# Local attention in a fused kernel: the third projection of values from step 14 to step 13, in another bank of PSUM

## The reference

```python
def _layer(x, wqkv, qs, ksc, wo, lg, lb, w1, b1, w2, b2):
    h = shift_token(x)
    q, k, v = jnp.split(h @ wqkv, 3, axis=-1)          # 8 heads of 64 each
    q = l2norm(q) * qs
    k = l2norm(k) * ksc
    q, k = rotary_xpos(q, k)
    o = local_attention(q, k, v)                       # window of 64: own block and the one before
    x = x + o @ wo
    h = shift_token(x)
    h = (h - mu) / jnp.sqrt(var + 1e-05) * lg + lb
    h = h @ w1 + b1
    a, g = jnp.split(h, 2, axis=-1)
    h = a * jax.nn.gelu(g, approximate=False)
    return x + h @ w2 + b2
```

## Time and profile before

| | |
|---|---|
| Runs | 4749.75, 4752.04, 4779.65 us |
| Profiled execution, its own time | 4754.64 us |
| Its span (first to last instruction) | 4752.8 us |
| Granted clock of TensorE, mean | 0.909 |
| Busy: PE, DVE, ACT, POOL | 4180.9, 3024.0, 2452.0, 1123.8 us |
| Chain that ended last: PE, DVE, ACT | 61%, 23%, 8% |

### The profile page before, as it was taken

The page is one execution under the profiler, slowest core; times in us unless marked ns, Lnnn a source line. Parts: engine busy times, 40 slices in busy tenths (PEclk is TensorE's granted clock), DMA queues, the critical chain, the costliest instruction groups (busy, mean ns, idle before and its releaser), DMA issues.

```text
span 4752.8 us, 62689 instructions
## 1 busy us (share of the span) xinstructions
PE 4180.9 (88%) x23278; PEld 1996.8 (42%) x23280; DVE 3024.0 (64%) x6690; ACT 2452.0 (52%) x4189; POOL 1123.8 (24%) x1579
## 2 busy tenths in 40 slices
PE   8888879999898889999886778989988989889999
PEld 5222335556522236555552235555553334333343
DVE  4888466777488867776346984666666653466622
ACT  3487634555348864554346543444444663236642
POOL 1100123333210013332113651111131013420034
PEclk8799988999779998998788998999987999969999
DMA  1100002111010011111000000000001000000000
GB/s 50 27 15 15 34 12 73 33 35 38 16 45 16 15 50 37 37 32 26 5 7 5 0 8 8 8 16 9 16 33 28 22 8 1 29 22 22 14 0 9
DMA packets 48017, 104.07 MB, mean 22 GB/s; under 512 B 15064, under 2 KB 15064, under 8 KB 46432
## 3 DMA queue, kind: packets, MB, share of 16 engines
q1 hardware_dynamic: 46560, 98.49, 7.6%
q10 hardware_dynamic: 1152, 1.57, 0.1%
HBM read 40.24 MB, written 1.05 MB: 9 GB/s over the span
## 4 chain that ended last, share of the span: by engine, by line
PE 61%; DVE 23%; ACT 8%; POOL 3%; issue 2%; DMA 1%; ACTq 1%; SPq 0%; POOLq 0%; DVEq 0%
PE PS L447 29%; PE PS L1123 8%; PE PS L1071 7%; DVE SM L1197 6%; PE PS L1103 3%; PE PS L2643 2%; DVE AR L2447 2%; ACT AR L454 2%; DVE AR L451 2%; PE PS L1756 1%; PE PS L1746 1%; PE PS L474 1%; PE PS L1076 1%; ACT AR L1171 1%; ACT PS L2391 1%
## 5 line engine op out<-in xcount | busy, mean ns | idle before, releaser
L1197 DVE TENSOR_REDUCE SM<-PS 128x1 f32<-128x512 f32 (+3 forms) x1792 | 1028.4, 626 | 242.7 <-PE PS L1071 161.9
L447 PE MATMUL PS<-AR,WS 128*128 128x512 f32 (+1 forms) x2112 | 1049.9, 636 | 76.2 <-DVE AR L451 30.3
L1171 ACT ACTIVATE AR<-PS 128x1024 f32<-128x1024 f32 (+3 forms) x896 | 825.5, 933 | 344.2 <-PE PS L1106 171.6
L454 ACT ACTIVATE AR<-PS 128x512 f32<-128x512 f32 (+4 forms) x728 | 440.1, 614 | 515.4 <-PE PS L447 387.9
L1071 PE MATMUL PS<-AR 51*128 51x512 bf16 (+3 forms) x1792 | 528.5, 392 | 142.1 <-DVE SM L1197 98.4
L447 PEld LDWEIGHTS PS<-AR,WS 128*128 128x128 f32 (+1 forms) x2112 | 400.1, 201 | 535.8 <-issue 407.2
L1827 ACT ACTIVATE AR<-PS,SM 128x128 f32<-128x128 f32 x512 | 229.6, 452 | 447.2 <-DVE SM L1890 443.2
L1123 PE MATMUL PS<-AR 128*32 128x512 f32 (+3 forms) x3584 | 452.2, 578 | 1.3 <-ACT AR L1171 0.9
L1071 PEld LDWEIGHTS PS<-AR 51*128 51x128 bf16 x1792 | 130.2, 94 | 662.6 <-DVE SM L1197 476.1
L1103 PE MATMUL PS<-AR 51*128 51x512 bf16 (+3 forms) x1792 | 388.1, 368 | 11.8 <-ACT AR L1171 11.0
L1230 POOL CAST MBT<-SM 128x8 bf16<-128x8 f32 x128 | 28.0, 219 | 1264.6 <-DVE SM L1201 1067.8
(11 more groups left out here) (323 smaller groups left out, 7153.8 us busy)
## 6 DMA issues: line engine op xcount, KB each, us to landing
TP<-RAW SPq DMA_DIRECT2D x512, 64.0 KB, 2.0
AR<-AR SPq DMA_DIRECT2D x720, 32.0 KB
WS<-wall SPq DMA_DIRECT2D x4, 3654.5 KB, 11.0
WS<-wall SPq DMA_DIRECT2D x8, 902.5 KB, 4.5
WS<-wall SPq DMA_DIRECT2D x2, 3334.5 KB, 10.5
WS<-wall SPq DMA_DIRECT2D x1, 2384.0 KB, 8.8
WS<-wall SPq DMA_DIRECT2D x1, 1543.5 KB, 6.0
AR<-AR ACTq DMA_DIRECT2D x48, 32.0 KB
```

Of the source, the lines that this page charges most:

```text
L447: t = e.matmul(o, l, r, start=(n == 0), stop=(n == len(pairs) - 1))
L454: return e.activation(o, i, ACT.Copy, scale=1.0)
L1171: e.activation(pv[:, :, off:512], sv[:, :, off:512], ACT.Exp, scale=scale).then_inc(*F.at_exp.up((s, u, p2)))
L1197: e.tensor_reduce(mh[:, at, k0 // 512:k0 // 512 + 1], bank(ring(n + g), m), AX.X, ALU.max, negate=True).then_inc(*F.at_max.up((s, k, i, rr ...
```

## The change

v2 moves, for g from 1 to 7, from the list `second` of step 14 to that of step 13, and it gets bank 4 where it had one of the ring. The ring is dealt over the remaining items as before. The projections of group 0, made ahead of the loop's attention, stay where they were.

```diff
-                second += [("v", g, j) for j, at in enumerate((8, 11, 14, 15) if g else (8, 11, 12, 12)) if n == at]
+                second += [("v", g, j) for j, at in enumerate((8, 11, 13, 15) if g else (8, 11, 12, 12)) if n == at]
...
         def l1f_banks():
             items = [x for u in SLOTS for part in l1f_dense(u) for x in part if x[0] not in ("norm", "ln", "back")]
-            return deal((5, 6, 7), items)
+            own = [x for x in items if x[0] == "v" and x[1] and x[2] == 2]
+            return {**deal((5, 6, 7), [x for x in items if x not in own]), **{x: 4 for x in own}}
```

## The result

| | before | changed |
|---|---|---|
| Median | 4757.21 us (11 runs, 4749.75 to 4779.65) | 4733.04 us (11 runs, 4720.02 to 4740.69) |
| Profiled execution, its span | 4752.8 us | 4737.0 us |
| Granted clock, mean | 0.909 | 0.912 |

The ratio of the times is 0.9934, 95% interval 0.9919 to 0.9948. By it the change saves 25 to 39 us, by the medians 24 us. The forecast was 4731 us, which is 21 us off the 4752.04 that the three runs of before gave; the kernel before, run more often, has 4757.

The account below looks back on a forecast made before the run. DVE usually waits for PE, but PE waits 1.55 us for DVE in step 14, then DVE 2.15 us for PE. Terms 17.8 + 2.2 + 1.2 = 21.2 us off 4752.04 give 4731; range 4714 to 4755, likeliest case 4727 to 4735.

Parts of the forecast that it names:

- v2 starts in step 13 without a wait, and its cost lies in the pause of w3: PE, step 13: v2 waits 0, takes at most 1.02 us, uses up the 0.92 us pause before w3; nothing late.
- The new wait for ACT's copy, margin 0.4 us: Step 14: ln (norm's transposes) waits in bank 4 for ACT's copy of v2, done 1067.0, ln due 1067.38; cost 0.
- gain in step 14: ln starts 1.68 us earlier; step 15's reduction on DVE comes 1.7 to 2.15 us earlier, 2.15 being the ceiling.
- Nine blocks at the full 2.15 (17.8 us): Nine blocks with w3's wait lose all DVE idle time in front of step 15's reduction, 17.8 of 27.5 us.
- first and third terms: First: 17.8 us of idle time in nine blocks; third: 1.2 us, three blocks whose lower clock lasts into step 0.
- Five blocks entering low at 0.45 each (2.2 us): Five blocks that enter step 13 at the lower clock gain 0.45 us each, 2.2 us together.
- rival A: All fourteen blocks gain in full as the lower clock goes there: 29 to 32 us, 4720; chance 0.17.
- What step 15 gains shortens the block.: After step 15 PE is the bound until the next step 12, so step 15's gain shortens the block.
- rival B: Gain given back: clock falls at other steps, more blocks enter step 13 low; 6 us saved, 4746; chance 0.17.
- The sum: Over both stages' fourteen blocks: 17.8 + 2.2 + 1.2 = 21.2 us saved.
- Rival D: Bank 4: ACT copies v2 late, ln starts 0.85 us later in 12 blocks; 10 us slower, 4762; chance 0.03.
- Rival C: Steps 14 and 15 thinner on PE, clock falls there and elsewhere; 19 us slower, 4771; chance 0.09.

Follow-up runs that it names:

- e4: Changed kernel with v2 (third projection of values) one step earlier, at step 12, still in bank 4; 4744.11 us, 0.997 of before.
- e1: Kernel before with v2 moved to step 13 but its bank left in the ring of three; 4802.38 us, 1.009 of before.
- e3: Kernel before with three unread matmuls in step 14's pause in front of w3 (fourth spreading); 4751.7 us, 0.9983 of before.
- e6: Changed kernel with v3 (fourth projection of values) moved from step 15 to step 14; 4757.94 us, 0.9992 of before.
- e8: Changed kernel with three unread matmuls added at the end of step 12 in blocks 0 to 6; 4728.19 us, 0.9926 of before.
- e2: Kernel before with v2 left in step 14 but given bank 4, out of the ring; 4794.39 us, 1.0072 of before.
- e5: Kernel before with seven unread matmuls in step 14's pauses, four before w3 and three before the transposes; 4749.7 us, 0.9972 of before.
- e7: As e4, plus seven unread matmuls in step 14 at the places of e5; 4742.39 us, 0.9958 of before.
- e10: Second run of e8's kernel, the changed kernel with three unread matmuls at the end of step 12; 4737.27 us, 0.9943 of before.
- e11: As e8, plus two unread matmuls each before v0 and the seventh item a in block 1 of each stage; 4720.16 us, 0.991 of before.

## Why the prediction was right, and where not

The median came within 2 us of the forecast, inside the range, and the signs by which it was to be known are there. Part of the closeness is luck. The forecast started from 4752, which further runs put at 4757, so the kernel before was 5 us slower than assumed and the saving larger than the 21 us summed: 24 by the medians, 25 to 39 by the ratio. The profiled execution saved less, 15.8 us of its span. Taken by its steps:

- **v2 starts in step 13 without a wait, and its cost lies in the pause of w3.** Right: no pause in front of w3 in any tail (e4 has none either). The condition was bank 4 (e1).
- **The new wait for ACT's copy, margin 0.4 us.** Right. The copy in block 5 (timeline of ACT) ends at 1118.9, ln starts at 1119.36; over both stages there is one wait of 0.4 us.

```profile
1118.30 0.59 ACT L454 ACTIVATE AR<-PS 128x512 f32<-128x512 f32 x1
```

- **The step "gain in step 14", 1.68 us of v2 taken out and 2.15 us as the ceiling.** The size held where the clock is at full: DVE's idle went from 2.15 to 0. The reason was mis-shared. Of the 2.15, 0.5 is the order's at full clock (e3, e6) and 1.6 the clock's. In other words v2 gains less by standing earlier than by what the clock does behind it: with v2 in step 13 it stays up or comes back sooner. e4 has it earlier still, closes the pause in front of w3 as well, and gets half. I had the lower clock as a remark in this step, and it was most of it.
- **Nine blocks at the full 2.15 (17.8 us).** The five even ones gained 1.2 to 1.8 us (block 4 of the first stage: 10.43 to 8.66), because the lower clock now lies on v2 and the start of step 14, and because an even tail takes 0.4 more at full clock too (e8: 8.19 and 7.78); the four odd ones gained 2.1 to 3.0 (block 5: 10.81 to 7.79). Together 19.4, where the first and third terms had 17.8 and 1.2.
- **Five blocks entering low at 0.45 each (2.2 us).** Too small: they gained 2.22, 1.65, 1.43, 0.12 and 1.41, 6.8 together. I had assumed that a block that entered low would do so again and stay low as long. The two with an odd number (2.22 and 0.12) now stand at 1.00 and come out of the long stretch. The other three do enter low again and gained 1.4 to 1.7 even so, since the clock is back before w3: in block 6 of the first stage w3 takes 0.38 us, where it took 0.60. That is part of rival A.
- **"What step 15 gains shortens the block."** Only in part. Blocks 3 and 5 of both stages have tails 2.1 to 3.0 us shorter, but the blocks are only 1.0 to 1.3 shorter, because the clock now falls in their steps 0 to 13. My argument against rival B, that steps 0 to 11 do the same work as before, held for the work and not for its clock.
- **The sum.** Tails 26.2 us against 21.2. Against that stands what rival B named, and I left out of the likeliest case: 5.7 us net lost again in the rest of the stages, 7.0 of loss in block 1 of the second stage and 6.3 in blocks 3 and 5 against gains in others. Too little gain at the tails and no loss elsewhere nearly cancelled.
- **Rival D.** Its place is real (e2), its price was not: I gave 10 us, which is the wait, where the run shows 35. **Rival C** did not come: the two stages' clock is 0.94 and 0.92, where it was 0.90 and 0.92.

With the numbers of the full clock the 144.4 us of before come apart: 112.6 us is what the tails take in the new order at 1.00 (e8), about 0.61 us x 12 = 7.3 more in the old order (e3, e5, e6; blocks 0 have nearly none), and the remaining 24.5 us is the lower clock. The change took the 7.3 and 19 of the 24.5. These shares hold with the clock restored first; the other way round the order's would be larger, as said at e3.

What stays open: what in PE's work makes the clock fall or stay up, since neither the length of the pause nor PE's busy time tells e4 from the changed kernel (of the 5.20 us up to the fall in e4's block 4 PE was busy for 4.57; at the same place it was 4.56 in e4's block 5 and 4.47 in the changed kernel's block 5, where the clock stayed at 1.00); why an execution falls into the long stretch of block 1 or not; and where the low stretches outside the tails will lie after a change.

## What to carry to other kernels

Where PE's pause is followed by matmuls at the lower clock, try several places for the work that can be moved, and read the clock at each: here one step further ahead the order was just as good and so was the pause, and the clock was not. Read the rest of the loop too, since what the moved stretch gains can be lost at steps that nobody touched (e6, e7). Give the moved work a buffer that is free at its new place, and check who else then waits for it: half a change (the step without the bank, the bank without the step) was 35 to 43 us slower than none. To learn what part of a gain is the clock's, compare stretches at a granted clock of 1.00 between kernels, block by block, and not the totals.

## What the runs showed of the hardware

- Short waits of PE cost more than their length. One of 0.78 us (e2) or 2.18 us (e1), put into a stretch of small matmuls, turned tails of 10.4 and 10.8 us into 13.5 and 13.9, with the granted clock down to 0.60 and 0.51.
- A busy PE does not by itself bring the clock back. Block 1 ran 30.72 us at 0.50 with PE busy for 30.63 of them. In the 6.69 us ahead of the fall, at 1.00, PE was busy for 5.61. Why it stays so long is open.
- Nor does the length of PE's pause alone say whether it falls: behind the same 0.64 us it fell in e4's block 4 and stayed at 1.00 in the changed kernel's block 5.
- Matmuls that nobody needs are a coin with two sides: at step 12, on PE's slack, they held the clock in 41 of 42 tails (e8, e10 and e11); in the pause of step 14 they held it in four (e3) or nine (e5) of fourteen, and where they failed they made the tail up to 3 us longer.
- ACT and DVE took the same time at either clock of TensorE (the reduction 0.42, the copy 0.59 and 0.60); among the rows shown only PE's own stretch.
